# An adaLN block on one core: LN1 from chunk 4 on works on transposed x, the mean is added by a transfer, kk's low part goes ahead of the residual sums, and buffers get other addresses

## The chip, the cores and the metric

The kernel runs on 1 core of one Trainium2 chip. The metric is device microseconds of one execution. Three runs of the kernel before took 967.29, 967.33 and 967.5 us; the median is 967.33.

## What is computed

x has 4 x 2048 tokens of 512 columns. Cut to what matters (mod is a modulation per batch, from c and wmod; all is float32):

```python
h = layernorm(x) * (1 + ca) + sa                  # LN1
omega = clip(softplus(h @ W_omega.T + b_omega), 1e-4, 100)
zeta = sigmoid(h @ W_zeta.T + b_zeta)
F = h @ W_B.T + b_B                               # A = omega**2, S = 1 / (1 + DT*DT*A), d = 1 - zeta
z, y = d*(S*z - DT*A*S*y) + Fz, d*(DT*S*z + S*y) + Fy   # a scan over the 2048 tokens
x = x + ga * ([z, y] @ C.T + h @ D.T)
h = layernorm(x) * (1 + cb) + sb                  # LN2
prev = h shifted by one token
r = sigmoid((mu_r*h + (1-mu_r)*prev) @ W_r.T)
k = (mu_k*h + (1-mu_k)*prev) @ W_k.T
out = x + gb * r * (relu(k)**2 @ W_v.T)
```

## The kernel before

The tokens are cut into 16 chunks of 512 (q; LN1, the projections and the scan work on a chunk) and 32 units of 256 (u; all behind the scan works on a unit). A pair of units, u even and u odd, belongs to one chunk. Each matmul operand is split into a high part (float32r, written by ACT) and a low part (what is left, written by DVE), and each product is three passes: high x high, high x low, low x high. So for h, mix_k, mix_r, kk and xs ACT writes the high part and DVE subtracts (`low`, L942).

Every engine has its order written out by hand; nothing but semaphores ties them. A pair in the main loop (u from 2 to 31, q = u // 2):

PE (L570 to L589). Both units: k product of u into ps_kr (L471; it waits on s_rt for tanh of unit u - 1, which reads the same banks, and on the high and low parts of mix_k), transposes of the LN2 output of u + 1 into ps_tv (L541; wait on s_rv, the read_out of u - 1). Even unit: the projections of chunk q + 2 into ps_pt, r product, h x D and states x C of unit u + 2 into ps_cd (`cd_product`). Odd unit: cd_product, then the first half of the LN1 transposes of chunk q + 3 (`t1_first_half`, L536, eight transposes at L346), r product, the second half (`rest_transposed_in`, L402). Last in both: v product of u.

ACT (L899 to L936). Both: relu of k, `shifted` (the part of the mixes that comes from the token before, L759), square and high part of kk, high part of mix_k. Even: `states_out` (L727; waits for all of the recurrence of chunk q + 1), tanh, high part of mix_r, `projections_out` (L698), softplus, `squared_angle`, `statistics2(u + 2)`, `normalise1(q + 3)` (L621: x_in times rstd plus bias, four tiles of 128x512). Odd: `h_blocks(q + 3)` for k = 0, 1 (L629: reads the transposed tiles out of ps_pt, times 1 + ca, plus sa, into h_full), `h_high`, statistics2(u + 2), high part of mix_r, tanh, h_blocks and h_high for k = 2, 3.

DVE (L1457 to L1513). The recurrence of a chunk is a generator of 65 small steps (L1102), `beside(rec, main, n)` takes n of them behind each instruction of main, `run(rec)` the rest, most of which wait for the step before. Even: read_out and add_out of u - 1, `statistics1(q + 3)` (L1042: bn_stats and bn_aggr on x_in, nine instructions), `mixes(u + 1)` (L972, L1011; the first waits on s_prev for ACT's shifted), `k_low(u)`, the rest of the recurrence, low parts of mix_k and of the states, gated_tanh, low part of mix_r, the first step of the next recurrence (L1111; waits on s_pev for ACT's projections_out), `residual(u + 2)` (L1016), read_out(u), `normalise2(u + 2)`, four more steps. Odd: add_out(u - 1), mixes(u + 1), residual(u + 2), k_low(u), low part of mix_k, h_low for k = 0, 1, low part of mix_r, normalise2(u + 2), gated_tanh, h_low for k = 2, 3.

POOL: rstd of LN1 (even unit, from DVE's statistics) and of LN2. SP: x_in of chunk q + 4 when the transposes of q + 3 are done (L310 to L313), x2 of unit u + 3, the store of u, and the gates' rows of the next batch.

Ahead of the loop stands a prologue with its own order: chunks 0 to 3 of LN1, units 0 and 1, the weights' high and low parts, the modulation. The statistics of chunks 1 and 2 are sums and squares on ACT (`sums1`, `squares1`), those of chunk 3 come from DVE.

Of the kernel before, what the change touches and what calls it, by code (L numbers as in the profile page):

```python
# [33 lines left out]

LAST = ((0, slice(0, D)), (1, slice(0, D // 2)), (1, slice(D // 2, D)))
# [5 lines left out]
def build(nc, d):  # L41
    ctx = ExitStack()
    with ctx:
# [6 lines left out]

        proj = [sb(f"proj_{n}", [P, KC, 256], F32R) for n in ("hi", "lo")]
# [4 lines left out]
        wv = [sb(f"wv_{n}", [P, KC, D], F32R) for n in ("hi", "lo")]  # L56
        ident = sb("ident", [P, P])
# [20 lines left out]
        neg_mean1 = sb("neg_mean1", [P, TPC])  # L78
# [4 lines left out]
        square_out1 = sb("square_out1", [P, 2, D], mybir.dt.bfloat16)  # L83
        square_out2 = sb("square_out2", [P, 2, D], mybir.dt.bfloat16)
        rstd1 = sb("rstd1", [P, TPC])
        h_full = sb("h_full", [P, KC, CHUNK])
        h = [[sb(f"h_{n}{i}", [P, KC, CHUNK], F32R) for n in ("hi", "lo")] for i in range(2)]

        x2 = sb("x2", [P, 4, TPU, D])
# [6 lines left out]
        mix_full = sb("mix_full", [P, 2, KC, UNIT])  # L96
        mix = [mix_full[:, n] for n in range(2)]


        with nc.sbuf_tensor("stage_mix", [P, 2, KC, D], F32) as stage_mix:  # L100
            pass
        mixs = [[sb(f"mix_{n}_{w}", [P, KC, UNIT], F32R) for w in ("hi", "lo")] for n in "kr"]
        with nc.sbuf_tensor("stage_kk", [P, KC, D], F32) as stage_kk:
            pass
        kks = [sb(f"kk_{m}", [P, KC, UNIT], F32R) for m in ("hi", "lo")]
        with nc.sbuf_tensor("stage_out", [P, KC, D], F32) as stage_out:
            pass
# [15 lines left out]
        xs = sb("xs", [P, CHUNK])  # L123
        xss = [sb(f"xs_{m}", [P, CHUNK], F32R) for m in ("hi", "lo")]
# [49 lines left out]
        s_xn1 = sem("s_xn1")  # L174
        s_t1 = sem("s_t1")
# [64 lines left out]
        def _(sp):  # L240
# [59 lines left out]
            for u in range(NUNIT):  # L300
# [9 lines left out]
                if s % 2 == 1 and u // 2 + 4 < NCHUNK:  # L310
# [1283 lines left out]
```

## Time and profile before

| | |
|---|---|
| median of the runs | 967.33 us |
| profiled execution | 966.77 us, its span 965.0 us |
| PE (matmul) busy | 933.3 us, 97% |
| DVE busy | 822.3 us, 85% |
| ACT busy | 691.9 us, 72% |
| POOL busy | 97.5 us, 10% |
| chain that ended last | PE 85%, DVE 7%, ACT 5%, DMA 1% |
| transposes for LN1 in the main loop and for chunks 2 and 3 (L346) | 224, 30.0 us busy |
| HBM traffic | 47.0 MB read, 16.8 MB written |

Busy time is the sum over an engine's instructions; it doesn't say what they wait for. Line numbers (L338) are those of the kernel before. PE's clock is given as a share of 2.4 GHz; its other level is 1.2 GHz.

### The profile page before, as it was taken

The numbers are of one execution on the slowest core, as the hardware profiler recorded it, in microseconds if no ns is written. First come the engines' busy times: TensorE is split into PE (matmuls) and PEld (weight loads), VectorE is DVE, ScalarE is ACT, GpSimd is POOL, SyncE is SP. The second block draws the span as 40 slices with busy tenths as digits, with TensorE's granted clock in tenths as the row PEclk, the third lists the DMA queues.
The fourth block names the chain that finished last, engine by engine and source line by source line (L and its number), as shares of the span: only waits on it lengthen the run. The fifth ranks groups of instructions, "written<-read, shape, count | busy, mean of one in ns | idle before, by whom it ended". The sixth has DMA issues, their size and how long they took to land.

```text
span 965.0 us, 14775 instructions
## 1 busy us (share of the span) xinstructions
PE 933.3 (97%) x5024; PEld 786.2 (81%) x5024; DVE 822.3 (85%) x2282; ACT 691.9 (72%) x1354; POOL 97.5 (10%) x117
## 2 busy tenths in 40 slices
PE   9995978899999999999999999999999999999998
PEld 3574867788888888888888888888888888888887
DVE  4897779798998989899997988899898889979664
ACT  4979766777868686886868687776867778766552
POOL 0001010010200201110020001001020101000000
PEclk9997998999999999999999999999999999999999
DMA  9810301021121302021131202112120211111001
GB/s 327 287 56 22 110 20 68 1 88 44 66 77 44 100 22 87 24 88 44 44 99 38 88 19 88 44 44 88 44 99 1 89 55 45 44 44 44 23 22 44
DMA packets 35435, 64.78 MB, mean 67 GB/s; under 512 B 3736, under 2 KB 4632, under 8 KB 35360
## 3 DMA queue, kind: packets, MB, share of 16 engines
q1 hardware_dynamic: 35360, 63.84, 19.5%
q8 instruction: 40, 0.66, 0.3%
q14 instruction: 35, 0.29, 0.1%
HBM read 47.02 MB, written 16.81 MB: 66 GB/s over the span
## 4 chain that ended last, share of the span: by engine, by line
PE 85%; DVE 7%; ACT 5%; issue 1%; DMA 1%; SPq 0%; ACTq 0%; DVEq 0%
PE ps_kr L338 33%; PE ps_cd L338 21%; PE ps_tv L338 17%; PE ps_pt L338 7%; PE ps_tv L379 3%; PE ps_pt L346 3%; ACT mix_full L759 1%; DMA stage_out<-in_wd 1%; PE ps_cd L386 1%; DVE mix_full L1011 1%; ACT x_in L625 1%; DVE tmp L1244 1%; DVE state L1248 0%; PE ps_tv L399 0%; DVE tmp L1168 0%
## 5 line engine op out<-in xcount | busy, mean ns | idle before, releaser
L1011 DVE SCALAR_TENSOR_TENSOR mix_full<-ps_tv,cur_m,mix_full 128x256 f32<-128x256 f32 x256 | 117.5, 477 | 31.4 <-ACT mix_full L759 31.3
L781 ACT ACTIVATE kk<-ps_kr 128x512 f32<-128x512 f32 x64 | 38.1, 599 | 124.2 <-PE ps_kr L338 123.9
L759 ACT ACTIVATE mix_full<-ps_tv,cur_m 128x255 f32<-128x255 f32 x256 | 120.1, 572 | 1.8 <-PE ps_tv L379 1.8
L1523 POOL TENSOR_SCALAR var<-sq 128x2 f32<-128x2 f32 (+1 forms) x34 | 43.0, 1265 | 633.7 <-ACT square_out L607 633.7
L338 PE MATMUL ps_kr<-mix_k_hi,wk_hi 128*128 128x256 f32 x512 | 81.0, 281 | 8.2 <-issue 8.2
L338 PEld LDWEIGHTS ps_kr<-mix_k_hi,wk_hi 128*128 128x128 f32 x512 | 71.3, 191 | 11.2 <-issue 8.8
L338 PE MATMUL ps_kr<-mix_k_hi,wk_lo 128*128 128x256 f32 x512 | 80.1, 279 | 0.0
L338 PE MATMUL ps_kr<-mix_k_lo,wk_hi 128*128 128x256 f32 x512 | 80.0, 279 | 0.0
L338 PE MATMUL ps_kr<-wr_hi,mix_r_hi 128*128 128x512 f32 x248 | 69.4, 402 | 4.8 <-ACT kk L781 4.8
L338 PEld LDWEIGHTS ps_kr<-mix_k_lo,wk_hi 128*128 128x128 f32 x512 | 69.0, 190 | 0.0
L338 PEld LDWEIGHTS ps_kr<-mix_k_hi,wk_lo 128*128 128x128 f32 x512 | 68.6, 190 | 0.0
L338 PE MATMUL ps_cd<-wd_hi,h_hi 128*128 128x512 f32 x248 | 68.1, 396 | 0.0
L338 PE MATMUL ps_kr<-wr_hi,mix_r_lo 128*128 128x512 f32 x248 | 67.7, 395 | 0.0
L338 PE MATMUL ps_kr<-wr_lo,mix_r_hi 128*128 128x512 f32 x248 | 67.7, 395 | 0.0
L338 PE MATMUL ps_tv<-wv_hi,kk_hi 128*128 128x512 f32 x240 | 67.6, 404 | 0.0
L338 PE MATMUL ps_cd<-wd_lo,h_hi 128*128 128x512 f32 x248 | 66.4, 390 | 0.0
L338 PE MATMUL ps_cd<-wd_hi,h_lo 128*128 128x512 f32 x248 | 66.4, 389 | 0.0
L773 ACT ACTIVATE mix_k_hi<-mix_full 128x512 fp32r<-128x512 f32 x64 | 40.6, 640 | 35.2 <-DVE mix_full L1011 34.7
L338 PE MATMUL ps_tv<-wv_lo,kk_hi 128*128 128x512 f32 x240 | 65.6, 396 | 0.0
L338 PE MATMUL ps_tv<-wv_hi,kk_lo 128*128 128x512 f32 x240 | 64.8, 392 | 0.0
L338 PEld LDWEIGHTS ps_kr<-wr_hi,mix_r_hi 128*128 128x128 f32 x248 | 46.2, 191 | 14.5 <-issue 5.0
L338 PEld LDWEIGHTS ps_kr<-wr_hi,mix_r_lo 128*128 128x128 f32 x248 | 47.1, 190 | 10.5
(236 smaller groups left out, 2255.0 us busy)
## 6 DMA issues: line engine op xcount, KB each, us to landing
x<-in_x SPq DMA_DIRECT2D x32, 512.0 KB, 3.7
out<-x SPq DMA_DIRECT2D x31, 512.0 KB, 2.8
x_in<-in_x SPq DMA_DIRECT2D x15, 1024.0 KB, 5.1
x<-in_wmod SPq DMA_DIRECT2D x3, 1024.0 KB, 7.3
mix_full<-in_wmod SPq DMA_DIRECT2D x2, 1024.0 KB, 9.2
x_in<-in_x SPq DMA_DIRECT2D x2, 512.0 KB, 5.4
stage_out<-in_wd SPq DMA_DIRECT2D x1, 1024.0 KB, 9.6
stage_mix<-in_wmod SPq DMA_DIRECT2D x1, 1024.0 KB, 10.8
```

Of the source, the lines that this page charges most:

```text
L338: mm = pe.matmul(out, act[a][k], weight[w][k], start=acc0 and a == 0 and w == 0 and k == 0, stop=acc1 and (a, w) == passes[2] and k == n - 1)
L346: mm = pe.transpose(ps_pt[:, k % 2, i * P:(i + 1) * P], x_in[:, i, k * P:(k + 1) * P], ident[:, :])
L379: mm = pe.transpose(ps_tv[:, k // 2, at:at + P], xn2[:, i, k * P:(k + 1) * P], ident[:, :])
L386: pe.matmul(bank, warm[:, 0:P], warm[:, :], start=True, stop=True)
L625: mm = act.activation(x_in[:, i, :], x_in[:, i, :], ACT.Identity, bias=norm_bias1[:, i:i + 1], scale=rstd1[:, i:i + 1])
L759: mm = act.activation(mix[n][:, k, 1:UNIT], ps_tv[:, j, c * UNIT:(c + 1) * UNIT - 1], ACT.Identity, bias=cur_m[:, SHIFT + k:SHIFT + k + 1] ...
L773: act.activation(mixs[n][0][:, 2 * j:2 * j + 2, :], mix[n][:, 2 * j:2 * j + 2, :], ACT.Identity)\
L781: act.activation(kk[:, i, :], ps_kr[:, i, :], ACT.Relu).then_inc(s_relu, 1)
L1011: dve.scalar_tensor_tensor(mix[n][:, k, :], ps_tv[:, j, c * UNIT:(c + 1) * UNIT], cur_m[:, alpha + k:alpha + k + 1], mix[n][:, k, :], ALU. ...
L1244: dve.tensor_tensor(t, node, frm.unsqueeze(1).broadcast_to([P, 2, 3, c]), ALU.mult)\
L1523: pool.tensor_scalar(var[:, :], sq[:, :], 1.0 / D, EPS, ALU.mult, ALU.add).then_inc(s_var, 1)
```

## The change

LN1 of chunks 4 to 15. The host hands in x once more, transposed (`xt`). The statistics of a chunk come from ACT: `sums1(q + 4)` at the end of an even unit (in the place of normalise1), `squares1(q + 4)` in the odd unit ahead of h_blocks; in the prologue both for chunk 4. x_in is loaded so that partition p holds four consecutive tokens, and POOL makes rstd from the squares. SP writes rstd and minus the mean to DRAM (`ln_out`), loads the next x_in, spreads the row of rstd over all partitions (`ln_in`) and loads the chunk of xt into h_full (`xt_in`, when h_low of the chunk before is done). POOL then issues two transfers that add the row of minus the mean to h_full (`centred`). DVE multiplies h_full by rstd in two instructions of 128x1024 (`normalised`), at the end of the even unit, and ACT's h_blocks read h_full in place of PSUM. So PE's LN1 transposes, ACT's normalise1 and DVE's statistics1 go away for these chunks. In the even unit four steps of the recurrence that stood at its end on DVE go too (they run later).

On DVE k_low(u) of the odd unit stands ahead of residual(u + 2). The buffers for ACT's squares, whose contents nobody reads, are now x_in, h, xn2 or rt, in float32, in place of two bf16 buffers of their own.

All buffers are laid out anew, with paddings of 224, 48 and 16 elements: weights, h, the states' parts and the large buffers start at multiples of 256 bytes, which none of the matmul operands did; mix_k's two parts start at 192 past one (64 past one before). The diff, cut:

```diff
-        proj = ...; ident = ...; ... (old order of the buffers)
+        sb("to_2048", [P, 224])
+        ... weights, h, xss; then
+        for n, pad in (("k", 48), ("r", 16)):
+            sb(f"to_mix_{n}", [P, pad])
+            mixs.append([sb(f"mix_{n}_{w}", [P, KC, UNIT], F32R) for w in ("hi", "lo")])
+        x_spread = d["x"].rearrange("(q p i) n -> q p i n", p=P, i=TPC)
+        xt_chunks = d["xt"].rearrange("(k p) (q t) -> q p k t", p=P, t=CHUNK)
+        ln_spread = ln_rows.rearrange("e n (p i) -> e p n i", i=TPC)
 # SP
+            def ln_out(q):
+                sp.wait_ge(s_rstd1, q + 1)
+                sp.dma_start(ln_spread[q % 2], ln_cols[:, :, :]).then_inc(s_ln_out, 16)
+            def ln_in(q):
+                sp.wait_ge(s_ln_out, (q - WIDE + 1) * 16)
+                if q > WIDE:
+                    sp.wait_ge(s_z, (q - WIDE) * 2)
+                sp.dma_start(ln_wide[:, :], ln_rows[q % 2, 0:1].partition_broadcast(P)).then_inc(s_ln_wide, 16)
+            def xt_in(q):
+                sp.wait_ge(s_h_lo, q * KC)
+                sp.dma_start(h_full[:, :, :], xt_chunks[q]).then_inc(s_xt, 16)
-                    sp.wait_ge(s_t1, q * KC)
-                    sp.dma_start(x_in[:, :, :], x_rows[q]).then_inc(s_xin, 16)
+                    ln_out(q)
+                    if q + 1 < NCHUNK:
+                        sp.dma_start(x_in[:, :, :], x_spread[q + 1]).then_inc(s_xin, 16)
+                    ln_in(q)
+                    xt_in(q)
 # PE
-                    if q + 3 < NCHUNK:
-                        t1_first_half(q + 3)
                     r_product(u, ps_kr if u + 1 < NUNIT else ps_tv)
-                    if q + 3 < NCHUNK:
-                        rest_transposed_in(q + 3)
 # ACT, before the loop
+            sums1(4)
+            squares1(4)
 # ACT, even unit
-                    if next_t1:
-                        normalise1(q + 3)
+                    if q + 4 < NCHUNK:
+                        sums1(q + 4)
 # ACT, odd unit, ahead of h_blocks
+                    if q + 4 < NCHUNK:
+                        squares1(q + 4)
 # DVE
+            def normalised(q):
+                dve.wait_ge(s_ln_wide, (q - WIDE + 1) * 16)
+                for j in range(2):
+                    k = slice(2 * j, 2 * j + 2)
+                    dve.wait_ge(s_centred[j], (q - WIDE + 1) * 16)
+                    dve.tensor_tensor(h_full[:, k, :], h_full[:, k, :],
+                                      ln_wide[:, :].unsqueeze(1).broadcast_to([P, 2, CHUNK]), ALU.mult)\
+                       .then_inc(s_z, 1)
+                    yield
 # DVE, even unit
-                    if next_t1:
-                        beside(rec, statistics1(q + 3), 1)
-                    else:
+                    if not next_t1:
                         run(rec)
...
-                    take(rec, 4)
+                    if next_t1:
+                        beside(rec, normalised(q + 3), 1)
 # DVE, odd unit
                     if next_mix:
                         beside(rec, mixes(u + 1), 1)
+                    beside(rec, k_low(u), 1)
                     if next_cd:
                         beside(rec, residual(u + 2), 1)
-                    beside(rec, k_low(u), 1)
 # POOL
+            def centred(q):
+                pool.wait_ge(s_xt, (q - WIDE + 1) * 16)
+                pool.wait_ge(s_ln_out, (q - WIDE + 1) * 16)
+                for j in range(2):
+                    pool.dma_start(h_full[:, 2 * j:2 * j + 2, :],
+                                   ln_rows[q % 2, 1:2].partition_broadcast(P).broadcast_to([P, 2, CHUNK]),
+                                   accum_op=ALU.add).then_inc(s_centred[j], 16)
-                if u % 2 == 0 and q + 3 < NCHUNK:
-                    rstd1_of(q + 3)
+                if u % 2 == 0 and WIDE <= q + 3 < NCHUNK:
+                    centred(q + 3)
+                if u % 2 == 1 and q + 4 < NCHUNK:
+                    rstd1_of(q + 4)
```

## Rows read from the trace of the kernel before

**Rows 1.** Table by stretches: length, busy time of each engine, clock, DMA share, GB/s.

```profile
323.48:379.13 55.65, 55.65 (x310) 48.15 (x310) 50.14 (x143) 41.99 (x82) 6.69 (x7) 1.00 0.20 62
824.36:878.24 53.88, 53.88 (x294) 46.50 (x294) 47.36 (x131) 34.41 (x70) 2.97 (x4) 1.00 0.11 40
```

**Rows 2.** Chain of work in order of time: start us, us, what; two k products.

```profile
353.14 5.47 PE ps_kr L338 x48
...
379.13 5.47 PE ps_kr L338 x48
```

**Rows 3.** Timeline of DVE, u = 8 and 9: start us, us, instruction, [idle before].

```profile
347.82 0.29 DVE L1111 TENSOR_SCALAR ze<-ze 128x256 f32<-128x256 f32 x1 [2.95 <-ACT f L694]
...
354.39 0.55 DVE L1038 TENSOR_SCALAR xn<-x,neg_mean,rstd 128x512 f32<-128x512 f32 x1
...
361.21 0.48 DVE L1011 SCALAR_TENSOR_TENSOR mix_full<-ps_tv,cur_m,mix_full 128x256 f32<-128x256 f32 x1 [1.47 <-ACT mix_full L759]
...
369.86 0.68 DVE L942 TENSOR_TENSOR kk_lo<-kk,kk_hi 128x512 fp32r<-128x512 f32 x1
```

**Rows 4.** Timeline of ACT, u = 8 and 9.

```profile
338.91 0.41 ACT L734 ACTIVATE xs<-state 64x256 f32<-64x256 f32 x1
...
353.20 2.92 ACT L625 ACTIVATE x_in<-x_in,norm_bias,rstd 128x512 f32<-128x512 f32 x4
...
365.70 0.63 ACT L773 ACTIVATE mix_k_hi<-mix_full 128x512 fp32r<-128x512 f32 x1 [0.18 <-DVE mix_full L1011]
...
369.81 0.20 ACT L616 ACTIVATE neg_mean<-sum 128x2 f32<-128x2 f32 x1 [0.42 <-DVE x L1030]
...
372.79 1.15 ACT L773 ACTIVATE mix_r_hi<-mix_full 128x512 fp32r<-128x512 f32 x2 [1.22 <-PE ps_kr L338]
...
375.25 1.09 ACT L803 ACTIVATE rt<-ps_kr 128x512 f32<-128x512 f32 x2
```

**Rows 5.** Timeline of ACT, u = 2 in the prologue's wake.

```profile
157.26 3.75 ACT L759 ACTIVATE mix_full<-ps_tv,cur_m 128x255 f32<-128x255 f32 x8
...
173.98 0.42 ACT L734 ACTIVATE xs<-state 64x256 f32<-64x256 f32 x1 [8.17 <-DVE state L1267]
```

**Rows 6.** Timeline of DVE, the same stretch.

```profile
161.88 0.48 DVE L1011 SCALAR_TENSOR_TENSOR mix_full<-ps_tv,cur_m,mix_full 128x256 f32<-128x256 f32 x1
...
170.39 0.38 DVE L1248 TENSOR_REDUCE state<-tmp 128x64 f32<-128x192 f32 x1
```

**Rows 7.** Timeline of ACT, chunk 1's sums and squares and what follows.

```profile
80.08 0.63 ACT L597 ACTIVATE x_in<-x_in 128x512 f32<-128x512 f32 x1
...
82.91 0.72 ACT L607 ACTIVATE square_out<-x_in,neg_mean 128x512 bf16<-128x512 f32 x1
...
85.74 3.73 ACT L759 ACTIVATE mix_full<-ps_tv,cur_m 128x255 f32<-128x255 f32 x8
```

**Rows 8.** DMA issues: what, queue, count, KB each, median us to landing.

```profile
x_in<-in_x SPq DMA_DIRECT2D x15, 1024.0 KB, 5.1
...
gate_a<-gate_rows SPq DMA_DIRECT2D x4, 256.0 KB, 4.7
```

**Rows 9.** Timeline of PE, the same stretch.

```profile
177.27 0.48 PE L338 MATMUL ps_cd<-wc_hi,xs_hi 128*128 128x512 f32 x1 [3.23 <-DVE xs_lo L942]
```

**Rows 10.** Table by stretches, behind two stops of PE.

```profile
177.30:182.30 5.00, 5.00 (x15) 4.00 (x16) 2.23 (x4) 4.92 (x12) 0.00 (x0) 0.66 0.00 0
128.00:133.00 5.00, 2.57 (x16) 1.90 (x15) 4.67 (x11) 3.91 (x6) 0.00 (x0) 1.00 0.00 0
```

**Rows 11.** Timeline of PE, r product and h x D of u = 8.

```profile
335.13 1.08 PE L338 MATMUL ps_kr<-wr_hi,mix_r_hi 128*128 128x512 f32 x4
...
340.63 1.07 PE L338 MATMUL ps_cd<-wd_hi,h_hi 128*128 128x512 f32 x4
...
346.07 0.39 PE L338 MATMUL ps_cd<-wc_hi,xs_hi 128*128 128x512 f32 x1
```

**Rows 12.** Timeline of POOL, u = 9.

```profile
371.65 3.65 POOL L1523 TENSOR_SCALAR var<-sq 128x2 f32<-128x2 f32 x1 [17.30 <-ACT square_out L607]
```

More of the change, by code:

```diff
@@ L33 @@
 EDGES = 2 + 3 * (UPB - 1)
+WIDE = 4
 LAST = ((0, slice(0, D)), (1, slice(0, D // 2)), (1, slice(D // 2, D)))
@@ L56, in build @@
         wv = [sb(f"wv_{n}", [P, KC, D], F32R) for n in ("hi", "lo")]
+        h = [[sb(f"h_{n}{i}", [P, KC, CHUNK], F32R) for n in ("hi", "lo")] for i in range(2)]
+        xss = [sb(f"xs_{m}", [P, CHUNK], F32R) for m in ("hi", "lo")]
+        with nc.sbuf_tensor("stage_mix", [P, 2, KC, D], F32) as stage_mix:
+            pass
+        mixs = []
+        for n, pad in (("k", 48), ("r", 16)):
+            sb(f"to_mix_{n}", [P, pad])
+            mixs.append([sb(f"mix_{n}_{w}", [P, KC, UNIT], F32R) for w in ("hi", "lo")])
+        with nc.sbuf_tensor("stage_kk", [P, KC, D], F32) as stage_kk:
+            pass
+        kks = [sb(f"kk_{m}", [P, KC, UNIT], F32R) for m in ("hi", "lo")]
+        with nc.sbuf_tensor("stage_out", [P, KC, D], F32) as stage_out:
+            pass
+        xn2 = sb("xn2", [P, TPU, D])
+        rt = sb("rt", [P, TPU, D])
+        kk = sb("kk", [P, 2, 2 * UNIT])
+        x_in = sb("x_in", [P, TPC, D])
+        h_full = sb("h_full", [P, KC, CHUNK])
+        x2 = sb("x2", [P, 4, TPU, D])
+        mix_full = sb("mix_full", [P, 2, KC, UNIT])
+        mix = [mix_full[:, n] for n in range(2)]
+        xs = sb("xs", [P, CHUNK])
+        gate_a = sb("gate_a", [P, D])
+        gate_b = sb("gate_b", [P, D])
+        ln_wide = sb("ln_wide", [P, CHUNK])
         ident = sb("ident", [P, P])
@@ L82, in build @@
         bn = sb("bn", [P, TPC, 2])
[L83 to L89, printed above, removed]
+        ln_cols = sb("ln_cols", [P, 2, TPC])
+        rstd1, neg_mean1 = ln_cols[:, 0], ln_cols[:, 1]
         sum2 = sb("sum2", [P, 2, TPU])
@@ L174, in build @@
         s_xn1 = sem("s_xn1")
+        s_ln_out, s_ln_wide, s_xt = sem("s_ln_out"), sem("s_ln_wide"), sem("s_xt")
+        s_centred, s_z = [sem(f"s_centred{j}") for j in range(2)], sem("s_z")
         s_t1 = sem("s_t1")
@@ L598, in sums1, with squares @@
                        .then_inc(s_sum1, 1)
-                act.wait_ge(s_sum1, q * TPC)
+                act.wait_ge(s_sum1, (q if q < 3 else q - 1) * TPC)
                 act.activation(neg_mean1[:, :], sum1[:, :], ACT.Identity, scale=-1.0 / D).then_inc(s_mean1, 1)
-            def squares(x, neg_mean, scratch, out, count, s_sq):
+            def squares(x, neg_mean, spare, out, s_sq):
                 for i in range(out.shape[1]):
-                    if count + i >= 2:
-                        act.wait_ge(s_sq, count + i - 1)
-                    act.activation(scratch[:, i % 2, :], x[:, i, :], ACT.Square, bias=neg_mean[:, i:i + 1],
+                    act.activation(spare[:, i, :], x[:, i, :], ACT.Square, bias=neg_mean[:, i:i + 1],
                                    accum_out=out[:, i:i + 1]).then_inc(s_sq, 1)
@@ L611, in squares1 @@
                 act.wait_ge(s_mean1, q + 1)
-                squares(x_in, neg_mean1, square_out1, sq1, q * TPC, s_sq1)
+                if q >= WIDE:
+                    spare = x_in
+                else:
+                    act.wait_ge(s_cd, (q - 1) * TPC)
+                    spare = h[q % 2][0]
+                squares(x_in, neg_mean1, spare, sq1, s_sq1)
             def statistics2(u):
@@ L618, in statistics2 @@
                 act.wait_ge(s_mean2, u + 1)
-                squares(x2[:, u % 4], neg_mean2[:, u % 2], square_out2, sq2[:, u % 2], u * TPU, s_sq2)
+                squares(x2[:, u % 4], neg_mean2[:, u % 2], rt if u == 1 else xn2, sq2[:, u % 2], s_sq2)
             def normalise1(q, tiles=range(TPC)):
```

54 lines of the change are left out of this document (28 added, 26 removed).

## The prediction, made before the changed kernel ran

> **What bounds the kernel now.** Four views were read, in this order. The table by stretches first: in a pair of units (u = 8 and 9, from 323.48 to 379.13 us) PE is busy for all of 55.65 us, while DVE is at 50.14 and ACT at 41.99; a late pair that has no transposes for LN1 (u = 26 and 27) takes 53.88, again all PE [rows 1]. So twelve pairs carry about 55.65 - 53.88 = 1.77 us of those transposes on the engine that sets the end. The chain of work, in order of time, gives the two marks that I count from: the k product of the even unit starts at E = 323.48, that of the odd unit at 353.14 (E + 29.66), the next even one at 379.13 [rows 2]. The timelines of DVE and ACT then show how far both run behind PE. They aren't full, but they are coupled: ACT starts to read the states out at 338.91 (E + 15.43), which was also when the recurrence ended, DVE waits 2.95 us for the projections that ACT brings out after that, and in the odd unit DVE reaches the mixes only 1.47 us before ACT has its half of them ready [rows 3, 4]. That coupling is what I follow below, for the PE product after it, k of the next even unit, may not start before tanh of the odd unit has emptied its bank.
>
> **The profile's own time.** Its span is 965.0 us, its execution took 966.77, and the median of the runs is 967.33. I sum differences against 966.77 and add 0.56 to come to the median.
>
> **PE loses 1.77 us a pair.** For chunks 4 to 15 that is 12 x 1.77 = 21.2 us, if nothing else ends later. Everything below is about what does.
>
> **DVE, even unit: statistics out.** Four bn_stats at 0.61 from start to start and five small ones at 0.1 to 0.2 go, some 3.2 us, ahead of the first mix. DVE can't use all of it: the first mix needs ACT's first half. In the odd unit that came at 361.21, 8.07 after the product's start, with DVE waiting [rows 3]; ACT does the same work in the even unit, so the first mix can't start before E + 8.07. But the nine steps of the recurrence that ran beside the statistics are still to be done, and two more, because four steps are taken beside the new multiply's place where now there are two. From E + 8.07 I count eight mixes at 0.39 and a copy (3.2), nine recurrence steps between them (1.6), two kk lows at 0.60 (1.2), and the last eight steps. These wait for one another: where they ran alone they took from 170.39 to 173.98, 3.6 us [rows 5, 6]. Together 9.6, less 0.1 where a step hides in a low: the recurrence ends at E + 17.5, which is 2.1 us later than 15.43. Removing DVE work makes the last result of the recurrence later. From both sides: if the last steps overlapped fully (0.2 each, 1.6 for 3.6) the end would be E + 15.6, if each waited as the last ones do, E + 18.5. I take 17.5, made of rows of the same steps.
>
> **Through ACT and back.** From the start of reading the states to DVE's first step of the next recurrence it is 347.82 - 338.91 = 8.91 us, all ACT [rows 3, 4], so that step moves from E + 24.34 to E + 26.4. DVE's work until LN2's second normalise and its two steps is unchanged: 354.39 + 1.33 - 347.82 = 7.90, to E + 34.3.
>
> **DVE, the new multiply.** Two tensor_tensor of 128x1024. The trace has none of that width; one of 512 takes 0.60 from start to start (0.68 long, the next starts 0.08 before its end) [rows 3], so 1024 takes between 0.60 (nothing for the width) and 1.20 (twice); I take 1.13, near the upper end, since the 256-wide mixes take 0.39. With two recurrence steps 2.66, where 0.8 was: 1.86 more. The six smaller recurrence steps that come next give 0.45 back. DVE reached the odd mixes at 361.21 - 1.47 = 359.74, E + 36.26. Now 36.26 + 2.1 + 1.86 - 0.45 = E + 39.8, or 10.1 after the odd product's start instead of 8.07. The cover of 1.47 us is gone and 2.0 us stay.
>
> **ACT.** In the even unit four normalise (2.92) [rows 4] become four sums and a mean (2.83), a draw [rows 7]. ACT ends them at about E + 34.6, relu's second half is due at E + 35.1: they just fit. In the odd unit squares1 adds 85.74 - 82.91 = 2.83 [rows 7], between mix_high and h_blocks. The write in float32 instead of bf16 I price at 0; the bounds are -0.1 and +0.2 each, as the spread between ACT forms of 512 (0.62 to 0.80). h_blocks reads SBUF: 0.71 each, as four of normalise, the same form, end 2.92 after they start with 0.80 for the last. The odd unit then goes: second mix_k high at 12.56 + 2.0 + 0.25 (larger steps between the mixes) = 14.8 after the product's start; then 0.55 for itself, squares 2.83, h_blocks 1.42, h_high 1.10, statistics2 1.76 (369.81 to 372.79 less the 1.22 wait), mix_r high and the table load 2.46, tanh 1.09 [rows 4]. The sum is 26.0. Without transposes PE would be ready at 379.13 - 353.14 - 1.77 = 24.2. So the k product waits 1.8 us for tanh, which had 2.8 us to spare before. The pair takes 29.66 + 26.0 + 0.05 = 55.7 us against 55.65. **What PE gives up is eaten**, in the eleven pairs that have squares1 (u = 3 to 23): +0.05 to +0.1 each, +1.1 by the upper. The twelfth (u = 24, 25) has none and gains 1.8.
>
> **kk's low part ahead of the residual sums.** Two lows, 0.60 each, and their two steps: 1.45. They end at 13.7 + 2.45 + 1.45 = 17.6 after the odd product's start; the v product is due at 18.5. In the old order they would end at 20.6, a stall of 2.1. Free here, and with it x2 is 1.45 later, at 20.55; statistics2 comes at 20.7 anyway. Queued behind them are mix_k's low, due at 24: free.
>
> **Transfers.** ln_out, x_in of the next chunk, ln_in and xt_in stand on SP ahead of the odd unit's store. The last waits for h_low, some 3 us into the next even unit, and the store's own wait (add_out) ends at about 6.5: no delay. On POOL the two adding transfers stand ahead of rstd2, which is due over 20 us later. The trace has no such transfer: 1 MB in takes 5.1 us, 256 KB spread from one row 4.7 [rows 8], so 1 MB of adding takes from 5 to 4 x 4.7 = 19 us; I take 10. Started near E + 9, it ends by E + 28 at worst, and the multiply stands at E + 34.3. Hidden.
>
> **Prologue.** sums1(4) and squares1(4), 5.66 us, come ahead of relu(2). They fill 2.6 us of ACT's waits, so shifted(3) starts at 160.3 instead of 157.26, the first mix at 162.4 instead of 161.88, and nine steps now run alone: 162.4 + 4.3 (mixes) + 1.7 (lows) + 1.55 + 5.95 = 175.9 against 173.95, +1.9 for PE, which already stood 3.23 us there [rows 5, 6, 9]. After that stop the granted clock was 0.66 over 5 us, that is partly at 1.2 GHz, while around one of 5.00 - 2.57 = 2.43 us it stayed at 1.00, 2.4 GHz [rows 10]. I add 0.7 (0 to 1.3). So +2.6. The 1.8 us stops above are shorter than 2.43 and should leave the clock alone.
>
> **Addresses.** 24 matmuls of r take 5.50 us, 24 of h x D 5.44 [rows 11], 2.5 ns apart each; their stationary operands start at different offsets in 256 bytes. If moving them saves 2.5 ns on r and v, that is 0.12 us a unit, seen only in the eight units where PE still bounds: -1.0. Bounds: 0 and -2.
> The Trainium skill (TensorE: Matmul & The Clock Gate, section on the missing 2.5 ns) gives N / 2.4 + 2.5 ns for a warm matmul, 215.8 ns at 512 columns. The 226.7 here is slower, and the page says nothing of addresses; if they are the difference, the sum would be that of the last rival.
>
> **Sum.** +1.1 - 1.8 + 2.6 - 1.0 = +0.9: 967.7 for the profiled execution, 968.2 at the median.
>
> **Rivals.**
> *PE stays the bound.* For it: DVE is at 90% and ACT would be at 82%, and a chain of 30 terms can be 1.8 us too long. Against it: it is built of durations, and the 1.47 and 2.8 us of cover are read, not guessed. It decides if tanh ends before 24.2. Then -21.2 + 2.6 - 3.5 (addresses in all units) = 945 to 957.
> *POOL falls behind DVE.* rstd1 moves to the odd unit, among DVE's sums and lows. A POOL operation on two elements a partition took 3.65 us at 371.65, while DVE ran lows [rows 12]. With rstd1 ahead of it rstd2 can end 1.2 later, normalise2 and read_out with it, from 5.0 to 6.2 us into the even unit, where the transposes are due at 5.5: +0.7 to 1.5 a pair, 976 to 985. It decides where rstd1 isn't done when DVE's two-source run begins.
> The Trainium skill (SBUF - State Buffer, Who interferes with whom) has the rule: a DVE instruction with two SBUF inputs blocks a GpSimd one that reads SBUF. The trace agrees with that by its 3.65 us. The same page warns that descriptors made on GpSimd wait beside DVE instructions in a two-port mode; no run here shows it, and the six us ahead of the multiply would cover it.
> *The clock falls* in the 1.8 us stops. The stop of 3.3 cost about 1.5; 11 x 1.5 gives 985.
> *Addresses speed all matmuls* towards 213.3 ns, the bare columns at 2.4 GHz. In a coupled loop that helps in the k product and the last units: 955.
>
> **Chances.** Forecast 0.56 (958 to 978: faster 0.17, same 0.17, slower 0.22), PE bound 0.19, POOL 0.14, clock 0.06, addresses 0.05. Faster by over 0.2% (about what a measurement can tell from no change) 0.41, within 0.2% 0.17, slower 0.42. The range 949 to 982 leaves out some 0.08 on each side.
>
> **What would show it.** Steps: no PE transposes for LN1 from chunk 4; the first even mix at E + 8.1; states read at E + 17.5; the odd mixes 10 us after the k product; tanh last before a PE stop of about 1.8 us ahead of each even k product. Wrong would be: pairs of 53.9 with no such stop; POOL above 1 us in rstd1 with PE stopped ahead of the transposes of xn2; a multiply that waits for its transfer.

## The result: 993.06 us, slower by 2.7%

| | before | after |
|---|---|---|
| median of the runs | 967.41 us (967.29 to 968.06, 4 runs) | 993.06 us (991.19 to 996.22, 4 runs) |
| ratio | | 1.0271, 95% interval 1.0256 to 1.0285 |
| profiled execution, span | 966.77, 965.0 us | 994.15, 992.4 us |
| mean granted clock of TensorE | 0.986 | 0.967 |

The forecast was 968.2 with a range of 949 to 982. The time is outside it, on the side of a rival that had been given 6 in 100, the clock falls in the stops, and beyond that rival's 985 too. First the page of the changed kernel: its engines' busy time, the engines' shares of the chain that ended last, and two transfers.

```profile
PE 929.2 (94%) x4832; PEld 783.9 (79%) x4832; DVE 818.3 (82%) x2198; ACT 720.7 (73%) x1510; POOL 104.0 (10%) x129
...
DVE 39%; ACT 28%; PE 23%; issue 9%; DMA 1%; SPq 0%; DVEq 0%; ACTq 0%
...
h_full<-in_xt SPq DMA_DIRECT2D x12, 1024.0 KB, 5.3
h_full<-ln_rows POOLq DMA_DIRECT2D x24, 512.0 KB, 6.9
```

TensorE is still busy for 94% of the span, but the chain runs through VectorE and ScalarE for two thirds of it. A high busy share hides what the table by stretches shows (columns: stretch, its length, busy time of each engine, granted clock, DMA). The first stretch is the pair of units 4 and 5, the others the pairs 8 and 9, and 10 and 11:

```profile
213.44:269.93 56.49, 54.16 (x292) 46.77 (x293) 49.63 (x136) 44.25 (x96) 7.47 (x8) 1.00 0.37 100
325.98:384.10 58.12, 55.64 (x292) 48.21 (x293) 49.94 (x137) 44.27 (x96) 7.47 (x8) 0.97 0.37 99
384.10:442.13 58.03, 55.59 (x292) 48.22 (x293) 49.72 (x137) 44.26 (x96) 7.46 (x8) 0.97 0.34 96
```

A pair took 55.65 us of 55.65 busy [rows 1]; now it takes 56.5 or 58.1, with 2.3 to 2.5 us in which TensorE stands, and "busy" TensorE time has grown from 54.2 to 55.6 between the first and the second row, at a clock of 0.97. TensorE's waits (releaser, us in total, times, longest) and the stops in order of time say where:

```profile
PE ps_kr L376 <- ACT rt L855: 26.9, 13, 2.5
PE ps_cd L376 <- DVE xs_lo L998: 7.1, 3, 5.2
```
```profile
213.44 0.71 PE L376 MATMUL ps_kr<-mix_k_hi,wk_hi 128*128 128x256 f32 x4 [1.29 <-ACT rt L855]
...
269.93 0.71 PE L376 MATMUL ps_kr<-mix_k_hi,wk_hi 128*128 128x256 f32 x4 [2.34 <-ACT rt L855]
...
325.98 0.71 PE L376 MATMUL ps_kr<-mix_k_hi,wk_hi 128*128 128x256 f32 x4 [1.85 <-ACT rt L855]
...
384.10 0.71 PE L376 MATMUL ps_kr<-mix_k_hi,wk_hi 128*128 128x256 f32 x4 [2.48 <-ACT rt L855]
```

From unit 4 to unit 28 every even k product waits for tanh, as forecast (13 times, 2 us each in the mean, where 1.8 was forecast). The second row is the states product that TensorE makes in units 2 and 28, for units 4 and 30: 5.2 and 1.25 us. What was not forecast stands in the microseconds behind the third of these stops:

```profile
325.98:326.98 1.00, 1.00 (x8) 0.95 0.24 90
326.98:327.98 1.00, 1.00 (x7) 0.50 0.00 0
...
329.98:330.98 1.00, 1.00 (x9) 0.85 0.38 82
330.98:331.98 1.00, 1.00 (x11) 1.00 0.87 231
```

The granted clock is 0.50, that is 1.2 GHz, for some 3.4 us of the product (three whole microseconds at 0.50 and parts of two), and its matmuls of 256 columns start 0.21 us apart there instead of 0.11. The k product of 48 matmuls takes 7.33 us; it took 5.47 before. That happens in ten even units, 8 to 26, behind stops of 1.85 to 2.50 us; it does not happen in units 4 and 6, behind stops of 1.29 and 2.34. So the length of the stop alone doesn't decide it. The Trainium skill (TensorE: Matmul & The Clock Gate, section "What's actually happening") has two states in its table, half and full clock; the trace agrees, with 0.50 and 1.00 in whole microseconds.

By the starts of the k products in TensorE's timeline the time goes as follows (after against before): +1.4 us up to unit 4 (213.44 for 212.01), +1.2 in the two pairs with the clock kept, +23.0 over the ten pairs with the fall (units 8 to 27), +1.8 in the last four units. Sum 27.4, the difference of the spans.

The chain's links in one pair (E = 384.10, the start of the even product; O = 415.29, that of the odd one), VectorE first, then ScalarE:

```profile
394.04 0.48 DVE L1067 SCALAR_TENSOR_TENSOR mix_full<-ps_tv,cur_m,mix_full 128x256 f32<-128x256 f32 x1 [2.42 <-ACT mix_full L811]
...
412.80 0.30 DVE L1178 TENSOR_SCALAR ze<-ze 128x256 f32<-128x256 f32 x1 [3.36 <-ACT f L746]
...
420.73 1.22 DVE L1121 TENSOR_TENSOR h_full<-h_full,ln_wide 128x1024 f32<-128x1024 f32 x1
...
422.06 1.22 DVE L1121 TENSOR_TENSOR h_full<-h_full,ln_wide 128x1024 f32<-128x1024 f32 x1
...
426.11 0.48 DVE L1067 SCALAR_TENSOR_TENSOR mix_full<-ps_tv,cur_m,mix_full 128x256 f32<-128x256 f32 x1
```
```profile
403.87 0.42 ACT L786 ACTIVATE xs<-state 64x256 f32<-64x256 f32 x1 [5.01 <-DVE state L1334]
...
430.93 0.63 ACT L825 ACTIVATE mix_k_hi<-mix_full 128x512 fp32r<-128x512 f32 x1 [2.60 <-DVE mix_full L1067]
431.47 0.71 ACT L649 ACTIVATE x_in<-x_in,ln_cols 128x512 f32<-128x512 f32 x1
...
439.61 1.28 ACT L855 ACT_TABLE_LOAD   x1
440.90 1.08 ACT L855 ACTIVATE rt<-ps_kr 128x512 f32<-128x512 f32 x2
```

They answer to [rows 3] and [rows 4]. The multiply that VectorE does on 1024 columns took 1.13 us from start to start with nothing behind but the next step (420.73 to 421.86), as estimated. Of VectorE's 2.42 us of waiting ahead of the first even mix the text below makes use.

### The profile page after: what moved, and what is told of

Same layout as the page of the kernel before. It is cut to its first block, busy times and chain, and to the rows that moved or that the text cites. A ratio compares the mean times of both kernels' runs of the same rounds, so it can differ in the third digit from the quotient of the medians.

```text
span 992.4 us, 14483 instructions
## 1 busy us (share of the span) xinstructions
PE 929.2 (94%) x4832; PEld 783.9 (79%) x4832; DVE 818.3 (82%) x2198; ACT 720.7 (73%) x1510; POOL 104.0 (10%) x129
## 4 chain that ended last, share of the span: by engine, by line
DVE 39%; ACT 28%; PE 23%; issue 9%; DMA 1%; SPq 0%; DVEq 0%; ACTq 0%
PE ps_kr L376 13%; DVE mix_full L1067 8%; ACT mix_full L811 4%; PE ps_cd L376 3%; PE ps_tv L376 3%; DVE h_full L1121 3%; ACT mix_r_hi L825 3%; ACT rt L855 3%; ACT x_in L649 3%; DVE x L1086 2%; DVE tmp L1311 2%; DVE tmp L1235 2%; DVE kk_lo L998 2%; DVE rt L1142 2%; ACT L855 2%
## 5 line engine op out<-in xcount | busy, mean ns | idle before, releaser
L376 PE MATMUL ps_kr<-mix_k_hi,wk_hi 128*128 128x256 f32 x512 | 87.7, 297 | 35.1 <-ACT rt L855 26.9
L376 PEld LDWEIGHTS ps_kr<-mix_k_hi,wk_hi 128*128 128x128 f32 x512 | 76.2, 204 | 42.0 <-issue 40.8
L1589 POOL TENSOR_SCALAR var<-sq 128x2 f32<-128x2 f32 (+1 forms) x46 | 32.6, 709 | 585.6 <-ACT xn L649 364.5
L376 PE MATMUL ps_kr<-mix_k_hi,wk_lo 128*128 128x256 f32 x512 | 88.4, 299 | 0.0
L376 PE MATMUL ps_kr<-mix_k_lo,wk_hi 128*128 128x256 f32 x512 | 86.7, 295 | 0.0
L376 PEld LDWEIGHTS ps_kr<-mix_k_hi,wk_lo 128*128 128x128 f32 x512 | 77.3, 210 | 0.0
L376 PEld LDWEIGHTS ps_kr<-mix_k_lo,wk_hi 128*128 128x128 f32 x512 | 74.4, 202 | 0.0
L825 ACT ACTIVATE mix_k_hi<-mix_full 128x512 fp32r<-128x512 f32 x64 | 39.7, 653 | 30.3 <-DVE mix_full L1067 30.3
L786 ACT ACTIVATE xs<-state 64x256 f32<-64x256 f32 x30 | 12.5, 417 | 64.6 <-DVE state L1334 64.5
L376 PEld LDWEIGHTS ps_kr<-wr_hi,mix_r_hi 128*128 128x128 f32 x248 | 46.8, 190 | 14.8 <-issue 5.0
```

The source lines that it names most:

```text
L376: mm = pe.matmul(out, act[a][k], weight[w][k], start=acc0 and a == 0 and w == 0 and k == 0, stop=acc1 and (a, w) == passes[2] and k == n - 1)
L825: act.activation(mixs[n][0][:, 2 * j:2 * j + 2, :], mix[n][:, 2 * j:2 * j + 2, :], ACT.Identity)\
L1589: pool.tensor_scalar(var[:, :], sq[:, :], 1.0 / D, EPS, ALU.mult, ALU.add).then_inc(s_var, 1)
```

## The experiments

Each is the kernel named with the edit shown. The kernel before ran beside them at 966.9 to 967.3 us.

**1. The clock by itself.** Work that nobody needs, in the place of the stop, in the changed kernel:

```diff
+                if u % 2 == 1 and 3 <= u <= 25:
+                    for _ in range(8):
+                        pe.matmul(ps_tv[:, 0, :], kks[0][:, 0, 0:P], wv[0][:, 0, :], start=True, stop=True)
                 for i in range(TPU):
                     v_piece(...)
```

> Eight matmuls of 512 columns (8 x 0.227 = 1.8 us), whose result is overwritten, stand ahead of the v product of each odd unit from 3 to 25, so that TensorE works through most of the 1.3 to 2.5 us in which it now waits for tanh. Theory (the stop itself costs little, the clock's fall behind it costs most): the stops shrink to 0.7 us or less, the granted clock of the even k product stays at 1.00, that product takes 5.7 to 5.9 us and not 7.33, and each of the ten pairs that had the fall takes 1.4 us less: 993.1 - 14 = 979. Rival (the lateness of the slow product is absorbed by waits of the coupled engines): 992 to 994. Rival (the v product's end is needed early by VectorE's read-out): slower, 995 or more.

Measured: 979.38 us (978.6 to 980.07). The pair of units 10 and 11, and its stop:

```profile
383.67:440.03 56.36, 55.82 (x300) 48.08 (x301) 48.84 (x133) 44.24 (x96) 7.46 (x8) 1.00 0.37 100
```
```profile
383.67 0.71 PE L376 MATMUL ps_kr<-mix_k_hi,wk_hi 128*128 128x256 f32 x4 [0.69 <-ACT rt L858]
```

13.7 us less, by doing more. The clock is 1.00, the even product no longer slow, the stop down to 0.69, the pair 56.36 for 58.03. tanh ends 26.6 us after the odd product's start as before (26.7), so the chain behind it hasn't changed. Over the ten pairs of units 8 to 27 the gain is 15.9 us, 1.6 a pair; 1.4 us of it are lost ahead of unit 4, whose product starts at 214.81 instead of 213.44. Half of the loss was the clock's fall, not the wait before it. The rival of an absorbed lateness is out.

**2. tanh first.** In ScalarE's odd unit (and on GpSimd, the root of LN2 ahead of that of LN1, not shown):

```diff
-                    if q + 4 < NCHUNK:
-                        squares1(q + 4)
                     ... h_blocks, h_high (0, 1)
+                    tanh(u)
                     ... statistics2(u + 2), mix_high(u + 1, 1)
-                    tanh(u)
                     ... h_blocks, h_high (2, 3)
+                    if q + 4 < NCHUNK:
+                        squares1(q + 4)
```

> Only ScalarE's order in the odd unit is changed: tanh directly behind the first half of h_high, then LN2's squares, mix_r high, the second half of h, and the squares of LN1 last (GpSimd takes rstd2 ahead of rstd1 to match). Theory (tanh, the last of ScalarE's chain, is what stops the even k product): tanh ends some 22 us after the odd k product's start and not 26.7, the stop goes, the clock stays at 1.00, pairs take 54.1 to 54.6 us and TensorE is the bound again: 951 to 958. Rival (VectorE's later recurrence is a bound of its own, whatever ScalarE's order): pairs stay above 55.7, 970 or more, with another wait in front of TensorE.

Measured: 971.41 us (969.91 to 974.04), far from the 951 to 958 of the theory. The stop at tanh is gone (from the odd k product to the next even one it is 24.2 to 24.3 us in every pair, where it was 26.8), but another has come in front of the transposes of xn2:

```profile
PE ps_tv L417 <- DVE rt L1142: 13.9, 10, 2.1
```
```profile
385.92 1.28 PE L417 MATMUL ps_tv<-ident,xn 128*128 128x128 f32 x8 [2.04 <-DVE rt L1142]
```
```profile
385.92:393.50 7.58, 7.58 (x31) 6.27 (x32) 6.93 (x30) 6.81 (x14) 0.00 (x0) 0.77 0.77 222
```

The transposes need the bank that VectorE reads out. Here is that read-out in the changed kernel, where the odd k product starts at O = 357.18, and in this one, where O = 353.78:

```profile
387.67 0.69 DVE L1142 TENSOR_TENSOR rt<-ps_tv,rt 128x512 f32<-128x512 f32 x1
```
```profile
384.30 0.68 DVE L1142 TENSOR_TENSOR rt<-ps_tv,rt 128x512 f32<-128x512 f32 x1
```

It is O + 30.5 in both. VectorE's chain hasn't moved; TensorE merely comes 2.6 us earlier and now meets it. The stop of 2.04 us there costs the clock as well (0.77 over the next 7.6 us). So tanh was what stopped TensorE, but VectorE's chain is as late and stops it at the next place: the rival was right in its main point, though pairs of 53.9 us are among those of up to 57.8.

**3. The recurrence first.** VectorE waits 2.42 us ahead of the first even mix while steps of the recurrence stand behind it:

```diff
+                    if next_t1:
+                        take(rec, 8)
                     if next_mix:
                         beside(rec, mixes(u + 1), 1)
```

> One line: in the even unit VectorE takes eight steps of the recurrence ahead of the first mix, in the 2.4 us in which it waits for ScalarE's shifted copies, and no more beside the mixes than before. Theory (the recurrence ends late because steps that were covered by the removed statistics now stand behind the mixes): ScalarE reads the states 3 us earlier, at 16.5 us and not 19.8 after the even product's start, everything behind it moves by as much, tanh ends at O + 24 or earlier, where O is the odd product's start, the stop ahead of the even k product is under 0.5 us, the clock stays, pairs take 54.1 us: 951 to 956. Rival (the squares of LN1 on ScalarE are the cause, not the recurrence): tanh moves by less than 1 us, 988 to 993 with the clock still falling.

Measured: 956.03 us (954.62 to 956.92), ratio to before 0.9884 (0.9869 to 0.9899), at the upper edge of the 951 to 956 of the theory. States read, the next even product and its pair:

```profile
391.42 0.42 ACT L786 ACTIVATE xs<-state 64x256 f32<-64x256 f32 x1 [1.02 <-DVE state L1334]
```
```profile
375.34 0.71 PE L376 MATMUL ps_kr<-mix_k_hi,wk_hi 128*128 128x256 f32 x4 [0.47 <-ACT rt L855]
```
```profile
375.34:429.65 54.31, 53.95 (x292) 46.59 (x293) 50.52 (x140) 44.49 (x96) 6.58 (x8) 1.00 0.36 103
```

One line is worth 37 us. The states are read at 375.34 + 16.1 instead of + 19.8 (+ 18.1 in experiment 1, where the clock stays too, so the line itself brings 2.0), tanh ends 24.6 us after the odd product's start instead of 26.6, the stop is 0.47 us with the clock at 1.00, and pairs take 54.0 to 54.6, the 53.88 of a pair without LN1's transposes [rows 1] and 0.1 to 0.7 more. The late end of the recurrence ("Removing DVE work makes the last result of the recurrence later") is shown to be the head of the loss: taking it back takes back the stops and, with them, the clock's falls.

**4. kk's low part put back** behind the residual sums, in the changed kernel, and **6. the same move alone** in the kernel before:

```diff
-                    beside(rec, k_low(u), 1)
                     if next_cd:
                         beside(rec, residual(u + 2), 1)
+                    beside(rec, k_low(u), 1)
```

> kk's low part of the odd unit is put back behind the residual sums, nothing else. Theory (the move was free or better): the v product of the odd unit now waits 2.0 to 2.5 us for kk's low part, TensorE reaches the even k product as late as tanh does, and the time is that of the changed kernel or longer, 993 to 1000. Rival (with the residual sums 1.45 us later LN2's squares on ScalarE, mix_r high and tanh are late, and that is the stop): the stop ahead of the even k product shortens by 1.4 us, the time falls to 975 to 985.

> The kernel before with one part of the change alone: kk's low part of the odd unit ahead of the residual sums. In the kernel before kk's low part ends 18.0 us after the odd product's start, the v product is due at 19 or later, and tanh has 2.8 us to spare of which the later residual sums take 1.5: 967.3 within 1. Rival (the two chains behind the residual sums are tight there too): 970 or more, with a stop ahead of the even k product.

Measured: 998.92 us (996.41 to 1001.68) without the move in the changed kernel, 967.18 us (ratio 1.0000, 0.9991 to 1.0009) with the move alone in the kernel before. Without it TensorE stops ahead of the v product:

```profile
PE ps_tv L376 <- issue: 29.7, 13, 2.7
```

The move is free where nothing is late and saves 5.9 us where the mixes are late, as the prediction had it ("in the old order they would end at 20.6, a stall of 2.1"; here 2.3 each). It saves no more than that because one stop replaces the other: TensorE's waits for tanh are gone in this run, and the clock falls behind the stop ahead of the v product instead, here in the odd unit of the pair from 390.71 (stretch, length, busy times, granted clock, DMA):

```profile
441.91:445.91 4.00, 4.00 (x11) 3.16 (x12) 3.92 (x9) 3.94 (x9) 2.20 (x2) 0.57 0.46 128
```

**5. The squares of LN1 nearly left out** (16 columns of 512, from chunk 5 on).

```diff
-                squares(x_in, neg_mean1, spare, sq1, s_sq1)
+                for i in range(TPC):
+                    act.activation(spare[:, i, 0:16], x_in[:, i, 0:16], ACT.Square,
+                                   bias=neg_mean1[:, i:i + 1], scale=5.6568542, accum_out=...)
```

> From chunk 5 on the squares of LN1 go over 16 of the 512 columns (scaled up to the same mean square), so they leave out nearly all of the 2.8 us that ScalarE spends on them in the odd unit; everything else is the changed kernel. Theory (two chains end together: behind the squares comes LN2's statistics, and its input, VectorE's second residual sum, is ready only 21.3 us after the odd k product's start): ScalarE waits 2 us for the sum in place of the squares, tanh ends at the same time within 0.3 us, the stops and the clock's falls stay: 988 to 994. Rival (what the prediction held: the squares are what makes tanh late): tanh 2 us earlier, no stop, clock at 1.00, 955 to 965.

Measured: 995.18 us (994.81 to 996.4), no better than with all squares. ScalarE now waits in their place:

```profile
439.08 0.20 ACT L672 ACTIVATE neg_mean<-sum 128x2 f32<-128x2 f32 x1 [1.59 <-DVE x L1095]
```

1.59 us for VectorE's second residual sum. Two chains end together, 21.4 us after the odd k product's start: ScalarE's (mix_k high, squares, h) and VectorE's (mixes, kk low, residual). Taking 2 us from one alone gives nothing. The changed kernel has a pair without these squares by itself, units 24 and 25, and there ScalarE waits in the same way:

```profile
842.50 0.21 ACT L663 ACTIVATE neg_mean<-sum 128x2 f32<-128x2 f32 x1 [2.75 <-DVE x L1086]
```

**7. tanh one place earlier**, on top of the one line of experiment 3; VectorE's low part of mix_r behind LN2's normalise and the gate.

```diff
+                    tanh(u)
                     if next_mix:
                         mix_high(u + 1, 1)
-                    tanh(u)
```

> The one-line kernel (eight steps of the recurrence ahead of the first even mix, 956.0) with, in the odd unit, tanh one place earlier on ScalarE, ahead of mix_r high, and VectorE's low part of mix_r behind LN2's second normalise and the gate, so that nothing urgent waits for the later mix_r high. Theory (the 0.5 us that are left ahead of each even k product are tanh's): the stop goes, ten times 0.5 us less and no start-up of the clock: 950 to 953. Rival (LN2's second transposes come late as in the order with tanh first, TensorE waits 0.5 to 2 us for the read-out of the v bank): 957 to 970.

Measured: 954.09 us (952.76 to 954.75), ratio to before 0.9861 (0.9846 to 0.9876): the lowest median of all, 39 us below the changed kernel and 13 below the kernel before. It is 2 us below experiment 3, which the noise doesn't separate: the intervals of the two ratios overlap. From unit 5 on it is 24.24 to 24.49 us from an odd to the next even k product, so tanh's stop is gone; from even to odd it is up to 30.3 where it was 29.6, with waits of up to 0.6 us for the read-out ahead of the transposes, the rival's place, so that less is won than the theory had.

**9. Both ends of the run**, on top of 7:

```diff
-                    if not next_t1:
-                        run(rec)
-                    if next_t1:
-                        take(rec, 8)
+                    take(rec, 8)
...
-            sums1(4)
-            squares1(4)
...
+                    if u == 2:
+                        sums1(4)
+                        squares1(4)
```

> The kernel with tanh ahead of mix_r high (954.1) and two more moves at its ends: in the last even units, too, eight recurrence steps go ahead of the mixes and the others beside them (before all steps ran alone there), and LN1's first sums and squares for chunk 4 stand behind relu, the shifted copies and mix_k high of unit 2, where ScalarE waits 9 us for the state. Theory (the stop of 1.25 us at 922.6 in the changed kernel and the 1.2 to 1.9 us that the states of unit 2 come late are both paid in full): the states of unit 2 are read 1.2 us earlier, TensorE's stop ahead of the states product of unit 30 goes: 950 to 952. Rival (the slow clock at both places, not the lateness, is what costs, and it stays): 953 to 955.

Measured: 962.76 us (961.79 to 965.16), 8.7 us slower than 7 and outside both expectations. Unit 3's k product does start earlier, at 182.33 instead of 186.12, but unit 4's starts at 215.38 instead of 211.52. GpSimd, and what TensorE waits for then:

```profile
182.87 1.40 POOL L1626 DMA_DIRECT2D h_full<-ln_rows  x1 [11.93 <-DMA h_full<-in_xt]
190.18 1.23 POOL L1626 DMA_DIRECT2D h_full<-ln_rows  x1 [5.91 <-issue]
191.49 0.18 POOL L1589 TENSOR_SCALAR var<-sq 128x2 f32<-128x2 f32 x1
```
```profile
193.86 1.94 PE L417 MATMUL ps_tv<-ident,xn 128*128 128x128 f32 x8 [5.71 <-DVE xn L1095]
```

With the squares of chunk 4 some ten microseconds later, the rows go out and xt comes in later, the first adding transfer is issued at 182.87 and the second 7.3 us behind it, and LN2's reciprocal root, next in GpSimd's order, waits for both: TensorE stops 5.71 us for the normalise, and the clock is at 0.50 behind it. That end loses 3.9 us. At the other end the stop of unit 30's states product became longer (3.35 us, 2.05 in experiment 7), with a fall of the clock behind it that experiment 7 doesn't have: from the k product of unit 28 to the next it is 29.54 us instead of 26.74. Neither edit paid.

**10. The adding transfers left out** of the changed kernel:

```diff
-                    pool.dma_start(h_full[:, 2 * j:2 * j + 2, :], ..., accum_op=ALU.add).then_inc(s_centred[j], 16)
+                    pool.sem_inc(s_centred[j], 16)
```

> The changed kernel with the two adding transfers of each chunk left out: GpSimd only counts their semaphores up, so LN1 from chunk 4 on lacks its mean. Theory (they end 8 us or more before VectorE's multiply and GpSimd has nothing urgent behind them): 991 to 994, the same stops of 1.3 to 2.5 us. Rival (their descriptors, their 7 us on GpSimd's queue or their traffic delay something): 985 or less.

Measured: 991.52 us (990.21 to 993.49) beside 993.06 (991.19 to 996.22), with the same waits for tanh:

```profile
PE ps_kr L376 <- ACT rt L855: 25.8, 13, 2.5
```

The transfers are hidden, as predicted: the medians are 1.5 us apart and the ranges overlap, so that no cost is shown, and the 8 us or more that the rival had are out. Two of the stops in this run say something of the clock:

```profile
270.00 0.87 PE L376 MATMUL ps_kr<-mix_k_hi,wk_hi 128*128 128x256 f32 x4 [2.28 <-ACT rt L855]
...
790.71 0.71 PE L376 MATMUL ps_kr<-mix_k_hi,wk_hi 128*128 128x256 f32 x4 [1.83 <-ACT rt L855]
```

They stand ahead of units 6 and 24. Behind the first the clock was 0.57 over 4 us, behind the second it stayed at 1.00. In the changed kernel it was the other way round: full behind 2.34 us ahead of unit 6, half behind 1.88 us ahead of unit 24.

**8, 11 and 12. The places of the buffers.** Three layouts: all buffers 128 bytes further and mix_k at 0 modulo 256, both on the one-line kernel, and the new layout alone in the kernel before.

```diff
-        sb("to_2048", [P, 224])
+        sb("to_2048", [P, 256])
```
```diff
-        for n, pad in (("k", 48), ("r", 16)):
+        for n, pad in (("k", 64), ("r", 16)):
```

> The one-line kernel (956.0) with the first pad 128 bytes longer, so that every buffer behind it starts 128 bytes further: weights and kk at 128 modulo 256, mix_r at 128, mix_k at 64 (as it was before the change) and no longer at 192. Theory (the place of the operands sets the rate: r and v gained 2.3 ns a matmul by the change, k lost 4.3 ns of 113.6 by mix_k at 192): the products of r and v go from 5.44 back to 5.50 us, those of k from 5.66 back to 5.46, net -0.08 us a unit, 953 to 955. Rival (k's longer time is not of its address but of the start behind a stop or of other engines' traffic): k stays at 5.66, r and v at 5.50, 958 to 960.

> The one-line kernel (956.0) with the pad ahead of mix_k 64 bytes longer: mix_k starts at 0 modulo 256 bytes instead of 192, mix_r and kk at 64 instead of 0, the weights stay at 0. Theory (a stationary operand at 64 modulo 128 costs 2.3 ns a matmul of 512 columns, as in the kernel before; 128 modulo 256 cost nothing): r and v go from 5.44 to 5.50 us each. If the moving operand's place sets k's rate, the k product falls from 5.66 to 5.46 us (net -0.08 us a unit, 953 to 955); if it does not, k stays at 5.66 and the time rises by 32 x 0.12 = 3.8 at most, 957 to 960.

> The kernel before with the changed kernel's places of all buffers (weights, h and xs at 0 modulo 2048, mix_r and kk at 0 modulo 256, mix_k at 192; the squares of LN2 leave their unused output in xn2 to make room), and nothing else of the change. TensorE bounds this kernel, so every ns of a matmul is seen. Theory (the places alone give the rates seen in the changed kernel: r and v 5.44 us for 5.50, k 5.66 for 5.47): +0.07 to +0.09 us a unit, 969 to 970.5. Rival (k's slower rate comes from something else in the changed kernel): k stays at 5.47, r and v at 5.44, 32 x 0.12 = 3.5 us less, 963 to 964.5. Rival (the places do nothing): 967 within 0.5.

Measured: 957.57 us (956.72 to 957.93), 963.21 (962.66 to 963.56) and 967.70 (967.22 to 968.33; ratio 1.0007, 0.9998 to 1.0016). The products in the chain (start, us, what, matmuls), of 12 and of 11; in 8 they are 5.66 (k), 5.44 and 5.44 (r and v):

```profile
335.19 5.44 PE ps_kr L340 x24
347.43 5.44 PE ps_tv L340 x24
352.87 5.66 PE ps_kr L340 x48
```
```profile
402.46 5.60 PE ps_tv L376 x24
408.06 5.75 PE ps_kr L376 x48
421.50 5.60 PE ps_kr L376 x24
```

The layout alone makes r and v faster by 0.06 us a product, as priced, and k slower by 0.19, which no term had; in a kernel bound by TensorE that is 26.06 + 29.68 for a pair of 25.99 + 29.66, 0.09 us a pair and about 1 us over the twelve. The medians, 967.70 and 966.87 beside it, say the same, but within the noise. Where the operands lie does change the rate, by up to 7 of 227 ns for a matmul of 512 columns. But "multiples of 256 bytes" is not the rule: 128 bytes further nothing changes, in either direction, and with mix_k on a multiple of 256 and mix_r and kk at 64 all three products are slower than in either kernel. Nor is it the place alone: in the changed kernel the matmuls of k start 0.118 us apart in every odd unit, where TensorE comes from the v product without a stop, and 0.114 us apart in nine of the thirteen even units that it enters from a stop (once the clock is back). In experiment 2, which has no stop there, they are 0.117 to 0.118 in all. Which distance between which operands decides, and what a stop changes about it, stays open.

## Why the prediction was wrong

| step of the sum | forecast | measured in the pair at E = 384.10 | in experiment 1, clock at 1.00, E = 383.67 |
|---|---|---|---|
| first even mix | E + 8.07 | E + 9.94 | E + 8.31 |
| states read | E + 17.5 | E + 19.77 | E + 18.13 |
| VectorE's first step after | E + 26.4 | E + 28.70 | E + 27.05 |
| multiply | E + 34.3 | E + 36.63 | E + 34.97 |
| first odd mix | O + 10.1 | O + 10.82 | O + 10.78 |
| second mix_k high | O + 14.8 | O + 15.64 | O + 15.59 |
| end of tanh | O + 26.0 | O + 26.70 | O + 26.64 |
| stop ahead of the even k product | 1.8 | 2.44 | 0.55, behind 1.8 of added matmuls |
| pair | 55.7 | 58.03 | 56.36 |

The two measured columns differ by the slow product: 1.6 us in each of the first four rows, and 1.6 from E to O (31.19 and 29.58). The last column against the forecast is the model's error: +0.2, +0.6, +0.6 and +0.7 in the first four rows. In the rows from O, 0.17 of +0.7, +0.8 and +0.6 is only a matter of reading: the prediction took O from the chain (353.14), these are the starts in the timeline, which has 352.97 for the same product.

- **"The 1.8 us stops above are shorter than 2.43 and should leave the clock alone"** is the step that failed: it put the clock's cost in ten pairs at nothing. One stop of 2.43 us with a full clock beside it [rows 10] was taken for a bound. The changed kernel has a stop of 2.34 us that leaves the clock at 1.00 and one of 1.85 that sends it to 0.50. Worth 13.7 of the 24.9 us between forecast and result (experiment 1). The rival that held this priced it at 1.5 a pair, and ten pairs with 1.6 each came; its chance was too small. That a stop recurs in each of eleven pairs should have raised it.
- **The pair was forecast 0.7 us too short even without the clock** (56.4 in experiment 1 for 55.7). The first even mix comes 0.24 later, as a k product behind a stop took 5.72 us at full clock and not 5.47, and from there to the states it is 9.8 us and not 9.4. The odd k product, 0.2 slower by the new layout, is not on this chain, since TensorE waits at its end. In eleven pairs this is 7 us: "+0.05 to +0.1 each" was the difference of two sums of thirty terms, and its error was larger than itself.
- **"The twelfth has none and gains 1.8"** failed. In units 24 and 25 the squares aren't there, and the pair took 58.16 (56.74 in experiment 1, with the clock at 1.00), where about 53.9 was forecast. The prediction had noted that the residual sums end at 20.55 and the statistics come at 20.7, and then took the squares away without asking what is late next. Experiment 5 shows the same for all pairs.
- **The recurrence** came as argued: removing work from VectorE made its last result later. It is the head of the loss, and experiment 3 takes 37 us away by one line there.
- **The chain from the states to tanh, tanh as releaser, the multiply at 1.13, the squares at 2.83**: right within 0.15 us a link.
- **kk's low part: free**, right (experiments 4 and 6). **Transfers hidden**, right (experiment 10 shows no cost); one transfer of 512 KB took 6.9 us to land, and the second is issued 7.5 us behind the first (335.17 and 342.63), so both took some 14 us where 10 was forecast, with the bounds 5 and 19. The Trainium skill (DMA: Bandwidth & Descriptors, section on the anatomy of one DMA on the SWDGE path) gives 2.0 us plus the bytes at 436 KB a us, an estimate of 3.2 us for 512 KB; the traces here have 6.9, so the measurement decides. Experiment 9 shows that the cover of "over 20 us" on GpSimd holds in the steady pairs only.
- **Prologue +2.6**: 1.9 came by unit 3 (187.73 for 185.81) and 1.4 by unit 4. **Addresses -1.0**: r and v as priced, k's 0.2 against it, net about +1 in the kernel before (experiment 12), within its noise.
- **POOL falls behind DVE** did not come: the list of TensorE's waits in the changed kernel has none for xn2. GpSimd's queue decided only in experiment 9, by the transfers and not by the roots.

Left open: what decides whether a stop of about 2 us costs the clock. Its length alone doesn't: the same two units had it the other way round in experiment 10 than in the changed kernel. It was not tried with stops of a set length.

## What to carry to other kernels

A removed operation may have been the cover under which a serial chain ran: look at what the engine did beside it and start that earlier, in the wait that the removal opens. A short stop that recurs on TensorE must be priced with the clock's fall behind it, here 1.6 us on top of 2; and if it can't be removed, useless matmuls in its place win that back. Before an operation is taken out of one chain, look for the second chain that ends at the same place.

## What the runs showed of the chip

- With TensorE busy for 55.6 of 58.0 us of a pair the clock still fell to 1.2 GHz behind single stops of 1.85 to 2.50 us, for about 3.4 us each time, and did not behind stops of 1.29 and 2.34 us in the same run, nor behind 1.83 us in experiment 10.
- 22 us of extra matmuls (8 x 0.227 in each of twelve odd units) made the kernel 13.7 us faster.
- Moving buffers in SBUF changed the rate of float32r matmuls between 226.7, 229.2 and 233.3 ns at 512 columns and between 114.0, 117.9 and 119.8 ns at 256 (5.47, 5.66 and 5.75 us for 48). With the new layout both 114 and 118 ns occur at 256 columns in one run.
- Of two adding transfers of 512 KB the second is issued 7.3 to 7.5 us behind the first (182.87 and 190.18, 335.17 and 342.63); GpSimd's next operation behind the second starts after 1.3 us (191.49).
